# One ready semaphore in place of two, and three edits to the order of work, in the last stage of a two-block transformer kernel

## The chip, the cores and the metric

The kernel runs on one core of a Trainium2 chip. The metric is the device time of one execution in microseconds (us).

The core has five engines with queues of their own: PE (matrix products; PEld is its weight load), DVE (vector work), ACT (activations and copies), POOL (further elementwise work, and here the issuer of transfers that add into memory) and SP (transfers). Each engine takes its instructions in order. They wait for each other by semaphores.

## The reference

x has 32 batches of 256 tokens of 128 features. Four blocks follow each other, each on the layernorm of x, each added to x: causal attention with 16 heads, a mixture of 16 experts, attention on hyperbolic distance, and a two-layer MLP. The change touches the last two:

```python
def _hyperbolic_distance(q, k, c):
    q_norm_sq = jnp.sum(q * q, axis=-1, keepdims=True)
    k_norm_sq = jnp.sum(k * k, axis=-1)[..., None, :]
    qk = jnp.einsum('bhnd,bhmd->bhnm', q, k)
    diff_sq = q_norm_sq + k_norm_sq - 2.0 * qk
    denom = (1.0 - c * q_norm_sq) * (1.0 - c * k_norm_sq)
    denom = jnp.maximum(denom, 1e-06)
    cosh_arg = 1.0 + 2.0 * c * diff_sq / denom
    cosh_arg = jnp.maximum(cosh_arg, 1.0)
    return jnp.arccosh(cosh_arg)
...
dist = _hyperbolic_distance(q, k, CURVATURE)
attn = jax.nn.softmax(-dist, axis=-1)
out = jnp.einsum('bhnm,bhmd->bhnd', attn, v)
...
h = jax.nn.relu(jnp.einsum('bsd,dw->bsw', x, w1) + b1)
return jnp.einsum('bsw,wd->bsd', h, w2) + b2
```

## The kernel before

Three stages run one after the other: causal attention, experts, and then hyperbolic attention with the MLP, in `hyperbolic_attention_and_mlp`. Only this last one changes. x stays in on-chip memory throughout.

The stage goes over the 32 batches. In each batch the 16 heads are taken as 8 pairs p = 0 to 7. One pair's matrix is 128 x 1024 numbers.

- Rows: DVE and ACT build feature rows from q and k (`dve_lo`, `dve_features`); PE turns them per pair (`pe_turn_rows`, L1362, "row r" below); ACT or DVE copies the result to `rowsT` (`copy_rows`, L1497), ACT for pairs 0 and 3.
- Products: `pe_pairs` (L1371) makes two products per pair from rowsT, the squared distance in `d_ps` and the inverse of the denominator in `i_ps`. Each is four matmuls of few rows, 28 for d and 6 for i, in different row groups of PE.
- DVE reads them: `dve_distances` (L1636) clamps d_ps into a ring `u` of 12 pairs, `dve_ratio` (L1641) multiplies by i_ps.
- The argument of arccosh then needs a square root. For pairs 0 to 5 POOL forms the product u(u + 2) in `spare` (`pool_product`, L1557 to L1560) and ACT takes its root (`act_roots`, L1504); for pairs 6 and 7 ACT takes two roots itself (L1508, L1509). POOL issues a transfer that adds the root into u (`pool_sum`, L1550). ACT takes logarithm and exponential one batch later (`act_weights`, L1517 and L1520), and PE multiplies with the values (`pe_values`, L1395).
- The output is normalised, projected and added to x two to three batches later (`pe_turn_o`, `dve_normalise`, `pe_project`, `dve_residual`). The MLP of a batch runs four to five batches later: `pool_norm4` (L1573) normalises x, `pe_turn_x4` (L1435) turns it, ACT copies both turned inputs at once (`act_both_xT`, L1478, "the xTs copy"), `pe_hidden` (L1445) makes the hidden layer in two halves, `act_relu` (L1545), `pe_y` (L1456) and `dve_y` (L1682).

No planner orders this. Each engine has a body per batch, written out by hand: a loop over p, with the other work hung on certain values of p. On PE, DVE and ACT batches 0 to 5 are written out, batches 6 to 29 are a hardware loop of three batches per pass, and 30 and 31 are written out again. POOL's list is written out in full. Constants say at which p the work stands: `HIDDEN_AT` for the two halves of the hidden layer, `SUMS_BEHIND` for the products behind which POOL issues the sums, and `BUSY_AHEAD` and `BUSY_BEHIND` for `pe_keep_busy` (L1424), products without use that go to a part of o_ps that is free.

In PE's body, at each p, come first the products of the next pair, then what else hangs on p. In the first step these are turn_x, turn_x4, rows 5 and 6, and at the end y. In ACT's body come a row copy, the xTs copy, the logarithms and exponentials of the batch before by pairs of p, with feature copies and relu between, and then the roots of this batch. A change of table (ACT_TABLE_LOAD) stands ahead of each half.

Of the kernel before, what the change touches and what calls it, by code (L numbers as in the profile page):

```python
# [23 lines left out]
TB = N // P  # L24
# [1210 lines left out]
def hyperbolic_attention_and_mlp(nc, io, keep, y_dram, batches):  # L1235
# [9 lines left out]
    RING = 12  # L1245
    TURN = 3
    PRODUCTS = (0, 1, 2, 3, 4, 5)
    SUMS_BEHIND = {5: (0, 1, 2, 3, 4, 5, 6, 7)}
    ROWS_BY_SCALAR = (0, 3)
    EARLY_ROWS = 5  # L1250
    VALUES_AT = (2, 3, 4, 5)
    BACK_AT, ATTN_AT, PROJECT_AT = 4, 6, 7
    HIDDEN_AT = (1, 3)
    BUSY_AHEAD, BUSY_BEHIND = {5: 1}, {4: 4, 7: 1}
    HW = WB // 2
    NORM_BEHIND, NORM4_BEHIND = 2, 5
    with ExitStack() as stack:
# [46 lines left out]
        xh_done, xh_turned, xT_done, qkv_ready = S_("xh_done3"), S_("xh_turned3"), S_("xT_done3"), S_("qkv_ready")  # L1304
        hi_done, qkv_taken = S_("hi_done"), S_("qkv_taken")
        norm2_done, gap_done = S_("norm2_done"), S_("gap_done")
        sides_done, inverse_done, masked_far_done = S_("sides_done"), S_("inverse_done"), S_("masked_far_done")
        inv_hi_done, rows_done, rows_turned, rowsT_done = S_("inv_hi_done"), S_("rows_done"), S_("rows_turned"), [S_(f"rowsT_done{n}") for n in range(2)]
        d_ready, i_ready, dist_done, u_done = S_("d_ready"), S_("i_ready"), S_("dist_done"), S_("u_done")
        raised = S_("raised")  # L1310
        prod_done, root_done, ln_done, w_done, pv_done = S_("prod_done"), S_("root_done"), S_("ln_done"), S_("w_done"), S_("pv_done3")
        sum_landed = [S_(f"sum_landed{n}") for n in range(HP)]
# [51 lines left out]

        def pe_pairs(pe, b, p, i):

            def products(ps, r0, n):
                for j in range(TB):
                    for e in range(2):
                        at = slice(e * PITCH + r0, e * PITCH + r0 + n)  # L1370
                        last = nc.tensor.matmul(ps[:, e * W2 + j * N:e * W2 + (j + 1) * N],  # L1371
                                                rowsT[at, slot(i, p), 1, j * P:(j + 1) * P],
                                                rowsT[at, slot(i, p), 0, :],
                                                start=True, stop=True)
                return last

            pe.wait_ge(rowsT_done[p % 2], b * (HP // 2) + p // 2 + 1)
            after(pe, dist_done, b * HP + p)
            products(d_ps, 0, DROWS).then_inc(d_ready, 1)
            after(pe, u_done, b * HP + p)  # L1380
            products(i_ps, IROW, IROWS).then_inc(i_ready, 1)

        def pe_values(pe, b, g, i):
            pe.wait_ge(w_done, b * HP + 2 * g + 2)
# [106 lines left out]

        def copy_rows(engine, b, p, i):
            engine.wait_ge(rows_turned, b * HP + p + 1)
            after(engine, i_ready, b * HP + p - RING + 1)
            dst = rowsT[:, slot(i, p), :, :].rearrange("p s n -> p (s n)")
            src = r_ps[p % 2][:, :]
            ins = nc.scalar.copy(dst, src) if engine is nc.scalar else nc.vector.tensor_copy(dst, src)  # L1497
            ins.then_inc(rowsT_done[p % 2], 1)
# [112 lines left out]
        def dve_features_end(dve, b):  # L1611
            vec = nc.vector
            dve.wait_ge(inverse_done, b + 1)
            vec.tensor_tensor(inverse, whole.unsqueeze(1).to_broadcast([P, 2, TB, 2, H]), signs[:, :, :, :, :], ALU.mult
                              ).then_inc(masked_far_done, 1)
            dve.wait_ge(masked_far_done, 2 * b + 1)
            for a in range(2):
                ins = vec.scalar_tensor_tensor(out=far[:, a, :, :], in0=signs[:, 1 - a, :, 1, :], scalar=BIG,
                                               in1=inverse[:, a, :, 1, :], op0=ALU.mult, op1=ALU.add)
            ins.then_inc(masked_far_done, 1)  # L1620
            at = lambda side, n: rows[:, side, :, :, IROW + n:IROW + n + 4:3]
            near = inverse[:, :, :, 0, :].rearrange("p a t h -> p t h a")
            there = far[:, :, :, :].rearrange("p a t h -> p t h a")
            vec.tensor_copy(at(0, 0), near)
            vec.tensor_copy(at(0, 1), near)
            dve.wait_ge(masked_far_done, 2 * b + 2)
            vec.tensor_copy(at(1, 0), there)
            vec.tensor_copy(at(1, 2), there).then_inc(inv_hi_done, 1)
            dve.wait_ge(inv_hi_done, b + 1)
            vec.tensor_tensor(at(0, 2), near, at(0, 0), ALU.subtract)  # L1630
            vec.tensor_tensor(at(1, 1), there, at(1, 0), ALU.subtract).then_inc(rows_done, 1)

        def dve_distances(dve, b, p, i):
            dve.wait_ge(d_ready, b * HP + p + 1)
            after(dve, pv_done, b * GROUPS + p // 2 - RING // 2 + 1)
            nc.vector.tensor_scalar(u[:, slot(i, p), :], d_ps[:, :], 0.0, None, ALU.max).then_inc(dist_done, 1)  # L1636

        def dve_ratio(dve, b, p, i):
            dve.wait_ge(i_ready, b * HP + p + 1)
            dve.wait_ge(dist_done, b * HP + p + 1)  # L1640
            nc.vector.scalar_tensor_tensor(out=u[:, slot(i, p), :], in0=i_ps[:, :], scalar=1.0 / DEN_MIN,  # L1641
                                           in1=u[:, slot(i, p), :], op0=ALU.min, op1=ALU.mult).then_inc(u_done, 1)
# [66 lines left out]
        with nc.Block() as block:  # L1709
            @block.tensor  # L1710
            def _(pe):
# [8 lines left out]
                def body(b, i, one_before, two_before, three_before, four_before, five_before, one_after, two_after):  # L1720
                    for p in range(HP):
                        following = next_pair(b, p, one_after)
                        if following:
                            pe_pairs(pe, *following, i if p + 1 < HP else (i + 1) % TURN)
                        if one_after and p == 0:
                            pe_turn_x(pe, b + 1)
                        if four_before and p == 0:
                            if not one_after:
                                pe.wait_ge(res_done, b - 2)
                            pe_turn_x4(pe, b - 4, (i - 4) % TURN, misc, N)  # L1730
                        if one_after and p == 1:
                            pe_qkv(pe, b + 1, 0)
                        for r in {0: (5, 6), 1: (7,)}.get(p, ()):
                            pe_turn_rows(pe, b, r)
                        if four_before and p == HIDDEN_AT[1]:
                            pe_hidden(pe, b - 4, 1, (b + 1) * (HP // 2))
                        if one_before and p in VALUES_AT:
                            pe_keep_busy(BUSY_AHEAD.get(p, 0))
                            pe_values(pe, b - 1, VALUES_AT.index(p), (i - 1) % TURN)
                        if one_after:  # L1740
                            if p == 2:
                                pe_qkv(pe, b + 1, 1)
                            for r in {5: (0,), 6: (1,), 7: (3,)}.get(p, ()):
                                pe_turn_rows(pe, b + 1, r)
                        if two_before:
                            if BACK_AT <= p < BACK_AT + TB:
                                pe_turn_o(pe, b - 2, p - BACK_AT, (i - 2) % TURN, b + 2 if one_after else batches)
                            if p == ATTN_AT:
                                pe_turn_attn(pe, b - 2)
                            if p == PROJECT_AT:  # L1750
                                pe_project(pe, b - 2)
                        if one_after:
                            for r in {6: (2,), 7: (4,)}.get(p, ()):
                                pe_turn_rows(pe, b + 1, r)
                        if one_before:
                            if p == HP - 1:
                                pe.wait_ge(o_copied, 2 * b)
                            pe_keep_busy(BUSY_BEHIND.get(p, 0))
                        if five_before and p == 0:
                            pe_y(pe, b - 5, 2 * (b - 1))  # L1760
                        if four_before and p == HIDDEN_AT[0]:
                            if not one_after:
                                pe.wait_ge(late_xT4_done, 1)
                            pe_hidden(pe, b - 4, 0, (b + 1) * (HP // 2))
                over_batches(pe, body)

                after(pe, res_done, END - 1)
# [138 lines left out]
            def _(dve):  # L1906
# [9 lines left out]
                def body(b, i, one_before, two_before, three_before, four_before, five_before, one_after, two_after):  # L1916
                    for p in range(HP):
# [4 lines left out]
                        dve_ratio(dve, b, p, i)  # L1922
                        if p == 0 and three_before:
                            dve_residual(dve, b - 3)
                        for r in {0: (4,), 1: (5, 6), 2: (7,)}.get(p, ()):
                            copy_rows(dve, b, r, i)
                        if p == 1 and five_before:
                            dve_y(dve, b - 5)
                        if p == 3 and three_before:
                            dve_stats(b - 3, i)  # L1930
                        if p == 4 and three_before:
# [163 lines left out]
```

## Time and profile before

| | |
|---|---|
| median of 3 runs | 2494.11 us (2487.18 to 2496.76) |
| the profiled execution | 2494.11 us; its span 2492.1 us, 2.0 us around it |
| third stage | from about 1338 us to the end |
| granted TensorE clock, mean | 0.91 of 2.4 GHz |
| busy over the whole span | PE 86%, DVE 78%, ACT 71%, POOL 65% |

A row of the timeline has the start in us, the duration in us, engine, line, operation, output and inputs with shapes, the number of instructions merged, and in brackets the idle time ahead of it with what ended it. Two long instructions of one engine overlap by about 0.1 us at their ends, so the starts, not the durations, give the pace. A row of a window has its ends and length, the busy time and instructions of PE, PEld, DVE, ACT and POOL, the granted clock as a share of 2.4 GHz, the busy share of the transfer engines and GB/s. "issue" is idle time for which the profile shows no semaphore.

### The profile page before, as it was taken

Reading aid. Unit: us, or ns where it says so; the run is one execution under the profiler, and the core shown is the slowest. Engines: PE = TensorE matmul, PEld = TensorE weight load, DVE = VectorE, ACT = ScalarE, POOL = GpSimd, SP = SyncE. Lnnn points to the kernel's source line nnn. Section 1 sums busy time; section 2 is a strip of 40 time slices with the busy share of each in tenths; the row PEclk is TensorE's granted clock in tenths of the full one; section 3 lists DMA queues with packets and bytes.
Section 4 is the critical chain, followed back from the end, with each engine's and each line's share of the span. In section 5 each row is a group of like instructions: output and inputs, shape, how many; then the busy total and the mean of one; then the engine's idle time right before and its main releaser. Section 6 shows DMA issues by size and latency. Waiting matters only on the chain. (4 is left out here: it accounts for less than half of the span.)

```text
span 2492.1 us, 50814 instructions
## 1 busy us (share of the span) xinstructions
PE 2147.4 (86%) x15438; PEld 1607.4 (64%) x15438; DVE 1950.1 (78%) x5939; ACT 1767.7 (71%) x3085; POOL 1626.9 (65%) x1866
## 2 busy tenths in 40 slices
PE   4999999999999988999996778877878787787876
PEld 3677777777777767888884445555555555554554
DVE  4677777777777765787776899988989898898982
ACT  2666666666666653444423999989889898998995
POOL 2766676676667730000005999989889898888992
PEclk7999999999999997999995788988889898888887
DMA  5000000000000004534430667756576566755674
GB/s 140 1 2 2 2 1 2 2 1 2 1 2 1 2 1 91 116 69 104 103 69 19 131 132 140 140 111 126 113 139 127 112 123 126 139 108 113 128 140 78
DMA packets 81422, 184.53 MB, mean 74 GB/s; under 512 B 9478, under 2 KB 31529, under 8 KB 81194
## 3 DMA queue, kind: packets, MB, share of 16 engines
q0 software_dynamic: 36864, 134.23, 28.7%
q1 hardware_dynamic: 36010, 43.38, 7.6%
q10 hardware_dynamic: 8320, 4.19, 0.7%
q8 instruction: 103, 1.69, 0.3%
q14 instruction: 125, 1.02, 0.1%
HBM read 42.85 MB, written 4.72 MB: 19 GB/s over the span
## 5 line engine op out<-in xcount | busy, mean ns | idle before, releaser
L1560 POOL TENSOR_TENSOR spare<-spare,u 128x1024 f32<-128x1024 f32 x192 | 456.0, 2375 | 16.0
L542 ACT ACTIVATE prob<-s_ps,nmax 128x128 f32<-128x128 f32 (+1 forms) x1024 | 364.3, 432 | 132.2 <-DVE nmax L599 132.2
L599 DVE CUSTOM_DVE_ANT_0 s_ps<-s_ps,mask 128x128 f32<-128x128 f32 (+1 forms) x1024 | 340.6, 385 | 100.6 <-issue 76.4
L1641 DVE SCALAR_TENSOR_TENSOR u<-i_ps,u 128x1024 f32<-128x1024 f32 x256 | 313.6, 1225 | 60.2 <-issue 31.9
L579 POOL TENSOR_TENSOR g_lo<-g_all,g_hi 128x512 fp32r<-128x512 f32 x256 | 329.2, 1286 | 21.4
L1636 DVE TENSOR_SCALAR u<-d_ps 128x1024 f32<-128x1024 f32 x256 | 311.3, 1216 | 34.4 <-PE d_ps L1371 32.2
L534 ACT COPY g_all<-g_ps 128x512 f32<-128x512 f32 x256 | 151.5, 592 | 161.2 <-PE g_ps L63 160.2
L1517 ACT ACTIVATE u<-u 128x1024 f32<-128x1024 f32 x256 | 257.0, 1055 | 3.5 <-DMA u<-spare 3.5
L1520 ACT ACTIVATE u<-u 128x1024 f32<-128x1024 f32 x256 | 255.5, 1050 | 0.0
L991 POOL TENSOR_TENSOR x_lo<-xTs,x_hi 128x512 fp32r<-128x512 f32 x16 | 21.8, 1360 | 326.9 <-ACT x_hi L987 326.9
L475 PE MATMUL t_ps<-ident,prob 128*128 128x128 f32 x1536 | 232.1, 274 | 1.6 <-ACT pT L609 1.2
L1395 PE MATMUL o_ps<-u,v 128*32 128x256 f32 x2048 | 157.5, 431 | 86.3 <-ACT u L1520 85.7
L1550 POOL DMA_DIRECT2D u<-spare x256 | 228.3, 1402 | 4.6 <-ACT u L1509 2.1
L475 PEld LDWEIGHTS t_ps<-ident,prob 128*128 128x128 f32 x1536 | 192.1, 141 | 55.6 <-ACT prob L542 2.0
L1362 PE MATMUL r_ps<-ident,rows 128*128 128x128 f32 x1024 | 186.0, 320 | 38.9 <-ACT rowsT L1497 30.9
L1371 PE MATMUL i_ps<-rowsT 6*128 6x256 f32 x1024 | 139.9, 354 | 92.2 <-DVE u L1641 91.4
L1558 POOL TENSOR_SCALAR spare<-u 128x1020 f32<-128x1020 f32 x192 | 215.8, 1124 | 0.0
L1159 ACT ACTIVATE act_g<-eg_ps 128x512 f32<-128x512 f32 x128 | 76.3, 598 | 189.8 <-PE eg_ps L63 189.7
L61 PE MATMUL s_ps<-g_hi,x_hi 128*128 128x512 f32 x384 | 188.6, 491 | 20.5 <-issue 16.7
L612 DVE COPY pT<-t_ps 128x512 f32<-128x512 f32 x256 | 176.6, 690 | 33.5 <-PE t_ps L475 27.2
L555 POOL TENSOR_TENSOR g_hi<-g_all,ones 128x4 fp32r<-128x4 f32 x256 | 51.6, 202 | 221.7 <-ACT g_all L534 218.2
L1504 ACT ACTIVATE spare<-spare 128x1024 f32<-128x1024 f32 x192 | 188.5, 1045 | 5.3 <-POOL spare L1560 5.3
(275 smaller groups left out, 5658.2 us busy)
## 6 DMA issues: line engine op xcount, KB each, us to landing
u<-spare POOLq DMA_DIRECT2D x256, 512.0 KB, 11.9
w_all<-w_rows SPq DMA_DIRECT2D x128, 256.0 KB, 5.9
x<-L_attn_x ACTq DMA_DIRECT2D x8, 512.0 KB, 13.9
y<-x SPq DMA_DIRECT2D x32, 128.0 KB, 9.9
wkqv<-L_attn_Wkqv SPq DMA_DIRECT2D x4, 528.0 KB, 8.7
gate_rows<-L_ffn_gate_proj SPq DMA_DIRECT2D x1, 512.0 KB, 14.4
up_rows<-L_ffn_up_proj SPq DMA_DIRECT2D x1, 512.0 KB, 11.5
down_cols<-L_ffn_down_proj SPq DMA_DIRECT2D x1, 512.0 KB, 13.2
```

The costliest lines, as they stand in the source:

```text
L61: nc.tensor.matmul(out, hi, other_hi, start=True, stop=False)
L475: last = nc.tensor.transpose(t_ps[s % 2][:, c * P:(c + 1) * P], prob[:, s % 3, c, :], keep.ident)
L542: last = nc.scalar.activation(prob[:, kind, at, :].rearrange("p c n -> p (c n)"), s_ps[kind][:, at.start * P:at.stop * P], ACT.Exp, bias=n ...
L579: nc.gpsimd.tensor_tensor(g_lo[:, gb, q, :], g_all[:, h % 2, :], g_hi[:, gb, q, :], ALU.subtract).then_inc(g_split, 1)
L599: last = nc.vector.tensor_tensor_reduce(out=scores, in0=scores, in1=keep.mask[:, N - width:N], scale=-1.0, scalar=3.4e38, op0=ALU.add, op1 ...
L1517: nc.scalar.activation(pair, pair, ACT.Ln, bias=1.0 if whole else 0.0).then_inc(ln_done, 1)
L1520: nc.scalar.activation(pair, pair, ACT.Exp, scale=-1.0 if whole else -2.0).then_inc(w_done, 1)
L1550: nc.gpsimd.dma_start(u[:, slot(i, p), :], spare[:, p, :], accum_op=ALU.add).then_inc(sum_landed[p], 16)
L1558: nc.gpsimd.tensor_scalar(extra[:, 4:2 * W2], pair[:, 4:2 * W2], 1.0, 2.0, ALU.mult, ALU.add).then_inc(raised, 1)
L1560: nc.gpsimd.tensor_tensor(extra, extra, pair, ALU.mult).then_inc(prod_done, 1)
L1636: nc.vector.tensor_scalar(u[:, slot(i, p), :], d_ps[:, :], 0.0, None, ALU.max).then_inc(dist_done, 1)
L1641: nc.vector.scalar_tensor_tensor(out=u[:, slot(i, p), :], in0=i_ps[:, :], scalar=1.0 / DEN_MIN, in1=u[:, slot(i, p), :], op0=ALU.min, op1= ...
```

## The change

The pair's two ready semaphores, `d_ready` and `i_ready`, become one, `pair_ready`. PE waits for both readers, `dist_done` and `u_done`, before the first of a pair's eight matmuls, and issues them in an order that takes the four row groups in turn. DVE waits once per pair, ahead of the distances. One semaphore that counted two events (`masked_far_done`) becomes two. POOL issues the sums of pairs 0 and 1 behind product 4 and not behind product 5. PE makes the first half of the hidden layer in step 2, ahead of the values, and no longer at the end of step 1. DVE does `dve_y` ahead of the copies of rows 5 and 6. The products without use become 10 calls per batch from 6.

```diff
-    SUMS_BEHIND = {5: (0, 1, 2, 3, 4, 5, 6, 7)}
+    SUMS_BEHIND = {4: (0, 1), 5: (2, 3, 4, 5, 6, 7)}
...
-    HIDDEN_AT = (1, 3)
-    BUSY_AHEAD, BUSY_BEHIND = {5: 1}, {4: 4, 7: 1}
+    HIDDEN_AT = (2, 3)
+    BUSY_AHEAD, BUSY_BEHIND = {3: 1, 5: 1}, {4: 6, 7: 2}
...
         def pe_pairs(pe, b, p, i):
 
-            def products(ps, r0, n):
-                for j in range(TB):
+            pe.wait_ge(rowsT_done[p % 2], b * (HP // 2) + p // 2 + 1)
+            after(pe, dist_done, b * HP + p)
+            after(pe, u_done, b * HP + p)
+            for j in range(TB):
+                for ps, r0, n in ((d_ps, 0, DROWS), (i_ps, IROW, IROWS)):
                     for e in range(2):
                         at = slice(e * PITCH + r0, e * PITCH + r0 + n)
                         last = nc.tensor.matmul(ps[:, e * W2 + j * N:e * W2 + (j + 1) * N],
                                                 rowsT[at, slot(i, p), 1, j * P:(j + 1) * P],
                                                 rowsT[at, slot(i, p), 0, :],
                                                 start=True, stop=True)
-                return last
-
-            pe.wait_ge(rowsT_done[p % 2], b * (HP // 2) + p // 2 + 1)
-            after(pe, dist_done, b * HP + p)
-            products(d_ps, 0, DROWS).then_inc(d_ready, 1)
-            after(pe, u_done, b * HP + p)
-            products(i_ps, IROW, IROWS).then_inc(i_ready, 1)
+            last.then_inc(pair_ready, 1)
...
         def dve_distances(dve, b, p, i):
-            dve.wait_ge(d_ready, b * HP + p + 1)
+            dve.wait_ge(pair_ready, b * HP + p + 1)
...
         def dve_ratio(dve, b, p, i):
-            dve.wait_ge(i_ready, b * HP + p + 1)
             dve.wait_ge(dist_done, b * HP + p + 1)
...
-                        if four_before and p == HIDDEN_AT[1]:
-                            pe_hidden(pe, b - 4, 1, (b + 1) * (HP // 2))
+                        if four_before and p in HIDDEN_AT:
+                            if not one_after:
+                                pe.wait_ge(late_xT4_done, 1)
+                            pe_hidden(pe, b - 4, HIDDEN_AT.index(p), (b + 1) * (HP // 2))
...
+                        if p == 1 and five_before:
+                            dve_y(dve, b - 5)
                         for r in {0: (4,), 1: (5, 6), 2: (7,)}.get(p, ()):
                             copy_rows(dve, b, r, i)
-                        if p == 1 and five_before:
-                            dve_y(dve, b - 5)
```

## Rows read from the trace of the kernel before

**Rows 1.** Busy time of each engine by window, one per pass of the loop.
```profile
1536.50:1636.60 100.10, 81.24 (x664) 55.81 (x662) 92.39 (x183) 96.25 (x124) 95.15 (x94) 0.93 0.69 131
...
1742.30:1848.10 105.80, 84.64 (x654) 58.79 (x654) 93.01 (x183) 96.25 (x124) 94.59 (x93) 0.89 0.65 123
1848.10:1952.20 104.10, 81.80 (x654) 56.40 (x654) 92.84 (x183) 96.19 (x125) 95.51 (x95) 0.92 0.66 125
...
sum 839.00, PE 670.04 PEld 463.22 DVE 745.18 ACT 770.00 POOL 760.78; mean PE 83.76 PEld 57.90 DVE 93.15 ACT 96.25 POOL 95.10
```

**Rows 2.** The same, one window per batch, between ACT's table loads.
```profile
1636.64:1675.76 39.12, 29.56 (x223) 20.62 (x224) 32.81 (x64) 32.12 (x42) 31.68 (x32) 0.87 0.59 112
1675.76:1708.35 32.59, 27.12 (x210) 18.80 (x210) 30.75 (x62) 32.02 (x42) 31.68 (x32) 0.88 0.70 133
1708.35:1742.33 33.98, 27.79 (x223) 19.27 (x222) 29.44 (x59) 32.12 (x42) 31.67 (x32) 0.91 0.67 127
```

**Rows 3.** Waits, 1500 to 2400 us: total us, times, longest.
```profile
ACT xTs L1478 <- PE misc L1435: 44.5, 14, 4.5
...
DVE u L1641 <- issue: 31.9, 7, 4.9
```

**Rows 4.** Timeline of DVE around the loop's jump back.
```profile
1633.08 1.22 DVE L1636 TENSOR_SCALAR u<-d_ps 128x1024 f32<-128x1024 f32 x1
1639.15 1.23 DVE L1641 SCALAR_TENSOR_TENSOR u<-i_ps,u 128x1024 f32<-128x1024 f32 x1 [4.86 <-issue]
```

**Rows 5.** One pass, 1638.9 to 1744.5: instruction packets; instructions of L1640.
```profile
q14 instruction: 5, 0.04, 0.1%
...
L1640 DVEq EVENT_SEMAPHORE  x24: 21/21/50, 1639.1 to 1736.4; - x24
```

**Rows 6.** Timeline of ACT, 1675 to 1712 us.
```profile
1690.25 1.99 ACT L1520 ACTIVATE u<-u 128x1024 f32<-128x1024 f32 x2
...
1697.55 4.83 ACT L1504 ACTIVATE spare<-spare 128x1024 f32<-128x1024 f32 x5
...
1702.75 1.05 ACT L1504 ACTIVATE spare<-spare 128x1024 f32<-128x1024 f32 x1
...
1710.67 0.59 ACT L1478 COPY xTs<-misc 128x512 f32<-128x512 f32 x1 [1.04 <-PE misc L1435]
```

**Rows 7.** Timeline of POOL, 1625 to 1712 us.
```profile
1672.10 2.79 POOL L1573 TENSOR_SCALAR xh<-x,part_mv,rstd 128x127 f32<-128x127 f32 x2
...
1694.16 2.36 POOL L1560 TENSOR_TENSOR spare<-spare,u 128x1024 f32<-128x1024 f32 x1
1696.85 0.20 POOL L1557 TENSOR_TENSOR spare<-u,twos 128x4 f32<-128x4 f32 x1 [0.33 <-DVE u L1641]
...
1700.47 5.31 POOL L1550 DMA_DIRECT2D u<-spare  x6
1704.69 2.78 POOL L1573 TENSOR_SCALAR xh<-x,part_mv,rstd 128x127 f32<-128x127 f32 x2
```

**Rows 8.** Timeline of PE, 1675 to 1698 us.
```profile
1675.91 0.38 PE L1435 MATMUL misc<-ident,xh 128*128 128x128 f32 x2
...
1677.00 1.95 PE L1456 MATMUL o_ps<-w,hidden 128*128 128x128 f32 x16
1678.88 0.39 PE L1371 MATMUL d_ps<-rowsT 28*128 28x256 f32 x2
...
1679.12 0.28 PE L1371 MATMUL i_ps<-rowsT 6*128 6x256 f32 x2
...
1693.90 3.55 PE L1424 MATMUL o_ps<-qkvoT,ident 128*128 128x256 f32 x8
```

**Rows 9.** Timeline of DVE in the same batch.
```profile
1678.46 1.28 DVE L1497 CAST rowsT<-r_ps 128x512 fp32r<-128x512 f32 x2
1679.65 0.41 DVE L1682 TENSOR_TENSOR x<-o_ps,x 128x256 f32 x1
...
1686.12 0.48 DVE L1668 BATCH_NORM_STATS2 part_stats<-x 128x6 f32 x2
```

More of the change, by code:

```diff
@@ L1306, in hyperbolic_attention_and_mlp @@
         norm2_done, gap_done = S_("norm2_done"), S_("gap_done")
-        sides_done, inverse_done, masked_far_done = S_("sides_done"), S_("inverse_done"), S_("masked_far_done")
+        sides_done, inverse_done, masked_done, far_done = S_("sides_done"), S_("inverse_done"), S_("masked_done"), S_("far_done")
         inv_hi_done, rows_done, rows_turned, rowsT_done = S_("inv_hi_done"), S_("rows_done"), S_("rows_turned"), [S_(f"rowsT_done{n}") for n in range(2)]
-        d_ready, i_ready, dist_done, u_done = S_("d_ready"), S_("i_ready"), S_("dist_done"), S_("u_done")
+        pair_ready, dist_done, u_done = S_("pair_ready"), S_("dist_done"), S_("u_done")
         raised = S_("raised")
@@ L1493, in copy_rows @@
             engine.wait_ge(rows_turned, b * HP + p + 1)
-            after(engine, i_ready, b * HP + p - RING + 1)
+            after(engine, pair_ready, b * HP + p - RING + 1)
             dst = rowsT[:, slot(i, p), :, :].rearrange("p s n -> p (s n)")
@@ L1614, in dve_features_end @@
             vec.tensor_tensor(inverse, whole.unsqueeze(1).to_broadcast([P, 2, TB, 2, H]), signs[:, :, :, :, :], ALU.mult
-                              ).then_inc(masked_far_done, 1)
-            dve.wait_ge(masked_far_done, 2 * b + 1)
+                              ).then_inc(masked_done, 1)
+            dve.wait_ge(masked_done, b + 1)
             for a in range(2):
@@ L1619, in dve_features_end @@
                                                in1=inverse[:, a, :, 1, :], op0=ALU.mult, op1=ALU.add)
-            ins.then_inc(masked_far_done, 1)
+            ins.then_inc(far_done, 1)
             at = lambda side, n: rows[:, side, :, :, IROW + n:IROW + n + 4:3]
@@ L1625, in dve_features_end @@
             vec.tensor_copy(at(0, 1), near)
-            dve.wait_ge(masked_far_done, 2 * b + 2)
+            dve.wait_ge(far_done, b + 1)
             vec.tensor_copy(at(1, 0), there)
@@ L1760, in body @@
                             pe_y(pe, b - 5, 2 * (b - 1))
[L1761 to L1764, printed above, removed]
                 over_batches(pe, body)
```

## The prediction

> **What bounds the kernel now.** I read the share of busy time by stretch first. The change touches only the third stage, 1338 to 2492 us. Of its 32 batches, b = 6 to 29 run in a hardware loop of three batches per pass, eight passes in 839.0 us [rows 1]. The first pass, which is entered without a jump back, takes 100.1 us; six of the other seven take 105.7 to 105.9 us and one 104.1 (of the eight rows the first, the third and the fourth stand). In a pass ScalarE (ACT) is busy 96.3 us, GpSimd (POOL) 95, VectorE (DVE) 93. So three engines are each near the length of the undisturbed pass, and none has much to give. Split by batch [rows 2], the batch behind the jump takes 39.12 us, the next 32.59, the third 33.98; ACT needs 32.0 to 32.1 in each. An undisturbed batch is therefore ACT's own work, end to end.
>
> Then the waits [rows 3]. DVE sits 31.9 us, seven times, at L1641 for "issue", that is for no semaphore. ACT waits 44.5 us for the transposes in front of its xTs copy, the largest part of it behind those seven. The DVE timeline shows the place [rows 4]: the last instruction of the pass starts at 1633.08, the first of the next pass only at 1639.15, 4.86 us idle. This is the jump back of DVE's loop. The DMA view has 5 instruction packets of 8 KB in one pass [rows 5], so the loop is fetched anew each pass. The compiled DVE loop has 340 instructions of 64 bytes, a packet carries 128. By the instruction that DVE had reached when each packet started, I place block edges at about its 57th, 185th and 313th instruction: the loop lies in four blocks, and its first block is gone when the jump wants it. ACT's loop (233 instructions) shows no such wait [rows 3].
>
> Last, the timelines of one undisturbed batch, all times from its row of ACT's second pair of exponentials, which ends at 1692.24 [rows 6]. POOL is busy without a gap but 0.3 us [rows 7].
>
> **The change part by part.**
>
> *The merged ready semaphore.* Each ratio loses one wait. The compiled list has a separate wait instruction in front of each of the 24 ratios of a pass [rows 5]; 18 of them vanish (six hold another wait too), and 42 vanish in the six batches written out ahead of the loop. The loop shrinks to 322 instructions and starts 42 earlier, so the edges move to about its 99th and 227th, and the third falls behind its end: three blocks in place of four. With the next block prefetched that makes four held at the jump. I take it that the 4.86 us stall goes. It is bounded by a pass without a jump: 105.8 - 100.1 = 5.7 us for six jumps and 104.1 - 100.1 = 4.0 for one, 38 us [rows 1]; I count 38. The lower bound of this gain is 0, if the block is lost all the same.
>
> The other side of the merge: PE now starts the d products of the next pair only when DVE's ratio has read i_ps. PE waits there anyway for the i products, so what follows on PE is not later: eight products together take about 0.5 us where both waits are met [rows 8], as four i products alone. For DVE the distances can start some 0.6 us after the ratio. In six of the eight steps a row copy or longer work lies between (two copies take 1.28 us); at p = 3 it is 0.48 us of statistics, at p = 5 about as much, so 0.1 to 0.2 us show [rows 9]. They are covered by the new DVE slack below; I count 0, and 0.3 x 26 = 8 us without that cover.
>
> *SUMS_BEHIND.* This is the costly edit. POOL's sums of pairs 0 and 1 move in front of its product 5. A sum waits for the root of its pair. Product 4 ends at 1696.5; root 0 starts at 1697.55 and, one of five in 4.83 us, ends at about 1698.6, root 1 at 1699.55 [rows 6, 7]. POOL now stands still 2.1 us, issues sum 0, waits for root 1, issues sum 1 (0.6 to 0.7 us each by six in 4.2), and only then multiplies. Product 5 used to run 1696.85 to 1700.5, now about 1700.3 (0.2 to 0.6 us more while descriptors are written) to 1704.4. Queued behind it on POOL: sums 2 to 5, norm4, sums 6 and 7, the products of the next batch. On ACT, root 5 stood at 1702.75 and must now wait until 1704.4: 1.7 us on the engine that sets the batch. On POOL, norm4 starts 3.9 us later less two sums already issued (1.4), so 2.5 us later; it ends at 1707.5 now, 1710.0 then. Its customer is turn_x4 on PE in the next batch's first step. In the batch before, norm4 was done at 1674.9 and turn_x4 ran at 1675.91 [rows 7, 8]: 1.0 us of slack, so 1.55 us remain, and PE's in-order queue behind it (rows 5 and 6, y, the next pair, qkv, hidden) and ACT's xTs copy go with it. The two delays run beside each other; the chain over PE and DVE is the longer. POOL stays out of the bound itself: its 31.7 us of work and the 2.1 us stand fit in 34.5.
>
> *dve_y ahead of the row copies.* y's products end at 1678.95 [rows 8]; DVE is through with the ratio of pair 1 at 1678.5 and used to copy two rows before y at 1679.65 [rows 9]. Now it waits 0.45 us for y with the copies behind it: distances 2 and all after, 0.5 us later. The last hidden product, and ACT's relu behind it, follow.
>
> *HIDDEN_AT.* Half 0 moves one step later on PE, into step 2. Half 1 remains behind pair 4. About 1.0 us of PE moves from a gap at p = 1 to p = 2, where qkv 1 comes about 1.5 us later than now, just as ACT reaches it. I count 0; without that cover 0.5 us a batch.
>
> *BUSY.* Four more calls a batch, two of them in step 4 on the way from the values to pair 6. The four there now take 3.55 us, most of it at the low clock [rows 8], so two more are 1.8 us, or about 1.0 at full clock. DVE gets distances 6 that much later, but by the first step of the next batch it waits for POOL's norm4 in any case (it would have 2 us of slack there). Count 0; bound 1.0 x 26 = 26 us. What they may give back is clock: 0.89 to 0.93 is granted in the passes shown [rows 1]. I count nothing, since PE also gets new waits.
>
> **The sum.** A fast batch: 1.55 + 0.5 = 2.05 us. In the third batch of a pass xTs already waits for a late PE (1.04 us at 1710.67), which hides part: 1.3. A pass: 2.05 + 2.05 + 1.3 = 5.4; eight passes +43. Jumps: -38. Batches 1 to 5, ACT nearly always at work there too: 1.5 x 5 = +7. Batches 30 and 31: +4; ACT's 1.7 us once more in the tail: +2. Sum +18, less 2 for clock kept up where the 5 us hole is gone: +16. The profiled execution itself took 2494.1 us (span 2492.1), which is also the median of the three runs. So 2510 us.
>
> **The rivals.**
>
> A. As above: jump cured, its gain eaten by the wait in front of product 5: 2485 to 2530.
>
> B. The jump still stalls. The edges are my reading and may lie some tens of instructions off, or the first block may be lost in any case. Then the 38 us are not won: about 2548. The Trainium skill, "Runtime: NRT & Kernel Launch", section "Instruction fetch mechanics", says that an engine holds two blocks of 256 instructions and that a taken branch out of this window costs a fetch. By that rule a loop of 322 can still reach over three blocks, and would then stay at this rival's time; the trace's packets are half that size.
>
> C. The end on the other side: POOL's stand before product 5 hides. It decides on one number: root 0 done at 1698.6 against product 4 at 1696.5. If POOL in steady state runs 2 us later against ACT, it does not stand, and what is left is two sums (1.3 us) ahead of product 5, which root 5 (2.2 us behind product 5's end now) takes without a wait. Then only y's 0.5 us x 26 = 13 us stands against 38: about 2470. For it: POOL is full in fast batches. Against: its cycle with the stand is still shorter than the chain's.
>
> D. The longer dummy work and the d products behind the ratio both show, with the low clock at every step 4: 26 + 8 on A: about 2544.
>
> **Numbers.** A 0.52, B 0.13, C 0.23, D 0.12. Half a per cent, 12.5 us, is what a measurement of this kernel can tell from none: 2481.6 to 2506.6. C is nearly all faster; of A 0.22 of the whole lies under 2506.6 with a little below 2481.6; the rest is slower. Faster 0.24, same 0.24, slower 0.52. Range 2470 to 2550: from C's time to B's. A's own is 2485 to 2530.
>
> **What would show it.** Stall: no "issue" idle at L1641 behind the jump, seven ACT waits of 4.5 us gone, passes all alike at 104 to 107 us. POOL: a new wait at L1550 for ACT's root of about 2 us in each batch, root 5 on ACT waiting 1 to 2 us for POOL. PE: turn_x4 waiting for POOL's norm4. DVE: y waiting about 2 us. Wrong: if passes are near 100 us (C), or show 4 us at the jump (B), or if DVE waits for d products far more than for y (D).

## The result: 3% slower, and the profile after

The change makes the kernel slower: 2568.57 us (median of 4 runs, 2557.45 to 2572.67) against 2494.95 us, ratio 1.0302, 95% interval 1.0263 to 1.034. Forecast were 2510 us and a range to 2550. The profiled execution took 2563.7 us, its span 2561.8. Two kernels below had one execution each in a slower state with a lower granted clock (a_hidden_back 3388 us, a_sums_back 3085 us); their ratios leave it out, and their medians would be at most 0.6 us lower without it.

Busy time by window, one per pass of the loop in the middle of the stage, answers to [rows 1]:

```profile
1653.23:1765.82 112.59, 91.28 (x679) 59.79 (x678) 93.59 (x184) 96.66 (x124) 94.77 (x94) 0.83 0.61 115
1765.82:1880.40 114.58, 92.48 (x674) 60.99 (x674) 93.15 (x183) 96.65 (x123) 94.75 (x94) 0.81 0.60 114
```

DVE, ACT and POOL do the same work as before (93, 96 and 95 us), but a pass takes 112.6 to 114.6 us and not 105.8; forecast were 104 to 107. PE's busy time grew from 84.6 to 91.3 us for 25 more instructions (the longer dummy work is 24 of them), and the granted clock is 0.83, not 0.89.

The waits, 1500 to 2450 us (total us, times, longest), answer to [rows 3]:

```profile
POOL u L1547 <- ACT spare L1501: 130.3, 26, 5.7
PE d_ps L1374 <- DVE u L1637: 116.5, 85, 2.4
DVE u L1633 <- PE i_ps L1374: 110.8, 67, 3.2
ACT rows L1485 <- PE misc L1350: 84.3, 25, 4.0
...
ACT spare L1501 <- POOL spare L1557: 40.7, 25, 3.5
DVE x L1678 <- PE o_ps L1453: 30.9, 26, 1.6
...
PEld misc L1432 <- POOL xh L1570: 2.4, 8, 0.3
```

DVE's idle time without a semaphore behind the jump [rows 3, 4] is gone from the list: the jump back is cured. But now ACT waits 3.4 us in each batch for qkv 1 (L1485), which it did not before, and DVE waits for pairs. The timeline of one batch shows where. PE first, from the end of step 1:

```profile
1729.61 1.95 PE L1453 MATMUL o_ps<-w,hidden 128*128 128x128 f32 x16
...
1732.75 0.66 PE L1362 MATMUL r_ps<-ident,rows 128*128 128x128 f32 x4
1735.83 0.58 PE L1374 MATMUL d_ps<-rowsT 28*128 28x256 f32 x2 [2.42 <-DVE u L1637]
...
1736.56 2.08 PE L1442 MATMUL r_ps<-xTs,w 128*128 128x256 f32 x4
1738.57 1.94 PE L1392 MATMUL o_ps<-u,v 128*32 128x256 f32 x16
1740.43 1.65 PE L1350 MATMUL misc<-qkvoT,xTs 128*128 128x384 f32 x2
```

Then the idle times that answer to it, one line each of the timelines of DVE, DVE, ACT, POOL and ACT:

```profile
1731.67 0.42 DVE L1678 TENSOR_TENSOR x<-o_ps,x 128x256 f32 x1 [1.06 <-PE o_ps L1453]
1742.73 1.23 DVE L1633 TENSOR_SCALAR u<-d_ps 128x1024 f32<-128x1024 f32 x1 [3.01 <-PE i_ps L1374]
1742.12 0.38 ACT L1485 ACTIVATE rows<-misc 128x256 fp32r<-128x256 f32 x1 [3.54 <-PE misc L1350]
1754.70 1.80 POOL L1547 DMA_DIRECT2D u<-spare  x2 [5.27 <-ACT spare L1501]
1760.21 1.06 ACT L1501 ACTIVATE spare<-spare 128x1024 f32<-128x1024 f32 x1 [1.55 <-POOL spare L1557]
```

DVE stands 1.06 us for y with two copies behind it, so pair 2 is late. PE stands 2.42 us for it with nothing to do, because the half of the hidden layer that used to fill this place has moved behind pair 3. Then pair 3, the half, values 0 and qkv 1 come one behind the other, each at nearly twice its time: 2.08, 1.94 and 1.65 us, where the same matmuls take 1.13, 1.07 and 0.91 in the kernel a_y_back (rows below). The windows of the hole and of what follows say why (the granted clock is the third number from the end):

```profile
1733.40:1735.80 2.40, 0.01 (x1) 0.00 (x1) 2.37 (x3) 2.40 (x6) 2.32 (x4) 0.91 1.06 201
1735.80:1742.00 6.20, 6.17 (x30) 2.81 (x30) 3.82 (x8) 2.78 (x3) 6.12 (x6) 0.50 0.77 153
```

0.50 is the lower level, 1.2 GHz. The batch is a typical one: between 1500 and 2420 us the hole is 2.42 us in all 25 batches, and from pair 3 to the end of qkv 1 PE takes 6.2 to 6.3 us in 22 of them and 4.8 to 5.0 in three.

### The profile page after: what moved, and what is told of

The parts are those of the page before. It is cut to its first block and busy times, and to the rows that moved or that the text cites. A ratio compares the mean times of both kernels' runs of the same rounds, so it can differ in the third digit from the quotient of the medians.

```text
span 2561.8 us, 51304 instructions
## 1 busy us (share of the span) xinstructions
PE 2204.0 (86%) x15686; PEld 1621.7 (63%) x15686; DVE 1956.0 (76%) x5939; ACT 1771.0 (69%) x3085; POOL 1622.4 (63%) x1866
## 3 DMA queue, kind: packets, MB, share of 16 engines
q0 software_dynamic: 36864, 134.23, 27.8%
## 5 line engine op out<-in xcount | busy, mean ns | idle before, releaser
L1374 PE MATMUL d_ps<-rowsT 28*128 28x256 f32 x1024 | 148.1, 367 | 160.0 <-DVE u L1637 157.1
L1374 PEld LDWEIGHTS d_ps<-rowsT 28*128 28x128 f32 x1024 | 94.3, 216 | 260.7 <-issue 256.2
L1392 PE MATMUL o_ps<-u,v 128*32 128x256 f32 x2048 | 170.3, 460 | 68.3 <-ACT u L1517 67.8
L1555 POOL TENSOR_SCALAR spare<-u 128x1020 f32<-128x1020 f32 x192 | 228.2, 1189 | 0.0
L1421 PE MATMUL o_ps<-qkvoT,ident 128*128 128x256 f32 x620 | 208.1, 480 | 0.0
```

Of the source, the lines that this page charges most:

```text
L1421: nc.tensor.matmul(o_ps[:, N:2 * N], keep.ident, keep.qkvoT[:, 0:2, :], start=True, stop=True, skip_group_check=True)
```

## Experiments

Theories ahead of the first runs. H: the moved half makes most of the loss. S: POOL's stand behind product 4 does. M: the merged wait, the dummy work or y does. "Before" ran at 2490.8 to 2492.4 us beside every group of kernels below, so their times are compared directly. Beside the changed kernel itself it ran at 2494.95, so differences to the changed kernel are uncertain by some 3 us more. Names that begin with a_ are the changed kernel with something put back; those with p_ are the kernel before with 72 extra instructions ahead of DVE's list (below, "the padded base") and one or more parts of the change added; those with b_ or m_ are what their sections say.

### Each part put back alone

```diff
 a_hidden_back
-    HIDDEN_AT = (2, 3)
+    HIDDEN_AT = (1, 3)
 a_sums_back
-    SUMS_BEHIND = {4: (0, 1), 5: (2, 3, 4, 5, 6, 7)}
+    SUMS_BEHIND = {5: (0, 1, 2, 3, 4, 5, 6, 7)}
 a_busy_back
-    BUSY_AHEAD, BUSY_BEHIND = {3: 1, 5: 1}, {4: 6, 7: 2}
+    BUSY_AHEAD, BUSY_BEHIND = {5: 1}, {4: 4, 7: 1}
```

> The changed kernel, with the first half of the hidden layer back at the end of PE's step 1. Theory H (the moved half is the main loss: it leaves a hole on PE at the end of step 1, the granted clock falls there, and pair 3, the half, the values and qkv 1 then run at the low clock in front of ACT's copy of qkv 1 and pair 4): 2500 to 2530 us, 40 to 65 under the changed kernel, ACT's 3.5 us wait for qkv 1 gone. Theory S (POOL's stand for root 0 is the main loss): within 15 us of the changed kernel, 2555 to 2570. Theory M (the merged wait, the dummy work or y's place is the main loss): the same as S here.

Measured: 2503.07 us, 65.5 under the changed kernel; ratio to before 1.0037 (1.0016 to 1.0058). As H said.

> The changed kernel, with all sums behind product 5 again. Theory H: the 5 us stand of POOL for root 0 goes, but little of the time, 2550 to 2568. Theory S: most of the loss goes, 2500 to 2530. Theory M: 2555 to 2570.

Measured: 2541.95 us, 26.6 under the changed kernel (1.0201, 1.0179 to 1.0222). Between H's and S's figures: a second cause, not the main one. ACT's wait for qkv 1 stays (81.0 us, 26 times).

> The changed kernel, with the dummy work of the kernel before (6 calls a batch, not 10). Theory H and theory S: 2545 to 2575, a few us either way by the clock. Theory M, if the dummy work in step 4 is what holds PE: 25 to 50 us less, 2520 to 2545.

Measured: 2572.01 us, 3.4 over the changed kernel (1.0323, 1.0306 to 1.0341). In the changed kernel the longer dummy work costs nothing in all. Why stands under "Parts together".

### The jump alone, and a base without it

```diff
+        pad = m.sb("pad", [P, 80])
...
+                for k in range(72):
+                    nc.vector.memset(pad[:, k:k + 1], 0.0)
                 dve.wait_ge(zeroed, 4)
                 for j in range(TB):
                     dve_lo(dve, 0, j, 0)
```

> The kernel before, with 72 one-element memsets on DVE ahead of the whole stage's list and nothing else, so that the DVE loop of 340 instructions starts 72 instructions later and lies in three blocks of 128 by my reading of the edges. If the jump's cost hangs on the blocks that the loop touches: the 4.9 us idle behind the jump goes, passes of about 100 to 101 us, 2450 to 2462 in all. If it hangs on the length of the loop, or the first block is lost in any case: 2490 to 2500 as before.

Measured: 2441.82 us, ratio 0.9793 (0.9775 to 0.9812): 49 us under before, by 72 instructions more, and 8 us under the range given. DVE's timeline over the jump answers to [rows 4], with no idle time:

```profile
1630.16 1.28 DVE L1498 CAST rowsT<-r_ps 128x512 fp32r<-128x512 f32 x2
1631.36 1.22 DVE L1637 TENSOR_SCALAR u<-d_ps 128x1024 f32<-128x1024 f32 x1
```

A pass, as a window:

```profile
1634.93:1733.91 98.98, 81.34 (x655) 55.88 (x656) 92.97 (x183) 96.15 (x123) 95.02 (x94) 0.91 0.69 131
```

The opposite test puts 60 such instructions into the changed kernel, so that its shorter loop straddles a fourth block.

> The changed kernel with 60 one-element memsets on DVE ahead of the stage's list, so that by my reading of the edges its loop of 322 instructions lies in four blocks again. If the edges decide: 4 to 5 us idle on DVE behind the jump, and 30 to 50 us more, 2598 to 2620. If the shorter loop was what cured the jump: 2560 to 2575.

Measured: 2586.32 us (1.0386, 1.0359 to 1.0412), 17.8 over the changed kernel and between the two ranges. The stall is back, 27.4 us in seven jumps, but costs less than I expected, since the passes hold other waits that take some of it up. DVE's timeline at the first jump, and its waits:

```profile
1648.84 1.21 DVE L1634 TENSOR_SCALAR u<-d_ps 128x1024 f32<-128x1024 f32 x1
1653.84 1.22 DVE L1638 SCALAR_TENSOR_TENSOR u<-i_ps,u 128x1024 f32<-128x1024 f32 x1 [3.78 <-issue]
```

```profile
DVE u L1638 <- issue: 27.4, 7, 5.3
```

So where the loop lies decides, not its length: 340 instructions run through, 322 stall. The merge cured the jump by moving and shortening the list, not as a semaphore. The transfer view agrees: between 1550 and 2300 us the instruction queue moves 43 packets in the kernel before and 39 in a_pad60, but 9 in b_pad72 and 9 in the changed kernel. The loop is fetched anew in each pass only where it stalls. None of the kernels below changes the count of DVE's instructions, and none of their traces shows the stall.

### Each part alone on the padded base

The edits are those of the change (the reverse of the diffs above; y as in the change's own diff).

> The padded kernel before (2441.8 us) with the first half of the hidden layer moved to step 2, nothing else of the change. Putting it back took 65 us off the changed kernel. If the move costs this alone, whatever stands beside it: 2495 to 2520 us, PE's low clock in step 2 and ACT's wait for qkv 1 of 2 to 4 us in each batch. If it costs only together with the merged wait or the sums (which make PE and ACT late already): 2440 to 2460.

Measured: 2460.20 us, +18.4 (ratio to before 0.9876, 0.986 to 0.9893). At the upper edge of the second range: alone it is a small part of the loss. What the half covers shows in the padded base, where PE makes it and then waits 0.60 us for pair 2's ratio (0 to 0.6 us in the other batches):

```profile
1672.12 1.03 PE L1446 MATMUL r_ps<-xTs,w 128*128 128x256 f32 x4
...
1674.19 0.50 PE L1372 MATMUL i_ps<-rowsT 6*128 6x256 f32 x4 [0.60 <-DVE u L1642]
```

With the half moved, PE's timeline in a batch:

```profile
1745.39 0.50 PE L1372 MATMUL d_ps<-rowsT 28*128 28x256 f32 x4 [0.52 <-DVE u L1637]
1746.72 0.50 PE L1372 MATMUL i_ps<-rowsT 6*128 6x256 f32 x4 [0.82 <-DVE u L1642]
1747.15 1.28 PE L1446 MATMUL r_ps<-xTs,w 128*128 128x256 f32 x4
1748.36 1.93 PE L1396 MATMUL o_ps<-u,v 128*32 128x256 f32 x16
1750.22 1.49 PE L1351 MATMUL misc<-qkvoT,xTs 128*128 128x384 f32 x2
```

The same pattern, shorter: the hole is 0.52 us and then 0.82, and ACT waits 1.58 us for qkv 1, not 3.54. It does not wait in every batch: 23.9 us in 16 waits between 1500 and 2400 us.

> The padded kernel before with DVE's y ahead of the copies of rows 5 and 6, nothing else. The prediction's step gives 0.5 us a batch, 13 us: 2450 to 2458. If DVE's copies have slack: 2438 to 2446.

Measured: 2469.57 us, +27.8 (0.9914, 0.9898 to 0.9931), twice the forecast and over both ranges. DVE's wait for y is 0.53 us in the batch shown, but 0.92 in the mean of 27 batches, the longest 1.6 (24.8 us, against 6.6 in the padded base, 1500 to 2400 us). The second relu on ACT waits 1.22 us here, where in a batch of the padded base it waited 0.66; together ACT's relus wait 34.8 us and not 15.0:

```profile
1711.70 0.42 DVE L1683 TENSOR_TENSOR x<-o_ps,x 128x256 f32 x1 [0.53 <-PE o_ps L1457]
1721.11 0.60 ACT L1546 ACTIVATE hidden<-r_ps 128x512 f32<-128x512 f32 x1 [1.22 <-PE r_ps L1446]
```

> The padded kernel before with the sums of pairs 0 and 1 behind product 4, nothing else. The prediction's own step gives 1.55 us a batch or 43 us: 2475 to 2490. What putting them back gave in the changed kernel, 27 us: 2460 to 2475. If POOL's stand hides: 2438 to 2447.

Measured: 2475.95 us, +34.1 (0.9947, 0.9928 to 0.9966). In the first range. POOL stands for the root (1.3 to 3.7 us, 1.9 in the mean) and ACT's root 5 for POOL (42.2 us in 26 waits):

```profile
1765.09 1.81 POOL L1551 DMA_DIRECT2D u<-spare  x2 [1.88 <-ACT spare L1505]
1770.60 1.06 ACT L1505 ACTIVATE spare<-spare 128x1024 f32<-128x1024 f32 x1 [1.56 <-POOL spare L1561]
```

> The padded kernel before with the dummy work of the change (10 calls a batch), nothing else. In the changed kernel the longer dummy work was worth nothing measurable, 3 us. The same here: 2438 to 2447. If it holds PE on the way to pair 6 in an undisturbed kernel: 2450 to 2470. If the clock it keeps up is worth something: 2425 to 2436.

Measured: 2479.56 us, +37.7 (0.9947, 0.9921 to 0.9972), over all three ranges and over the prediction's bound of 26. PE behind step 4 (twelve products, six calls), PE behind step 7 (four products, two calls, ahead of the next batch's first step), and ACT, which has to wait for the turned inputs:

```profile
1732.88 3.04 PE L1425 MATMUL o_ps<-qkvoT,ident 128*128 128x256 f32 x12
...
1745.69 1.73 PE L1425 MATMUL o_ps<-qkvoT,ident 128*128 128x256 f32 x4
```

```profile
1748.64 0.59 ACT L1479 COPY xTs<-misc 128x512 f32<-128x512 f32 x1 [1.20 <-PE misc L1436]
```

In the mean of the batches, the products behind step 4 take 3.0 us here and 2.5 in the padded base (there 1.9 to 3.5), and those behind step 7 take 1.7 and 0.9. ACT's waits for the turned inputs grow from 8.3 to 29.8 us and those of the relus from 15.0 to 21.5.

```diff
 b_merge: the changed kernel with half, sums, dummy work and y all put back
```

> The changed kernel with all four edits of the order (hidden half, sums, dummy work, y) put back, so that of the change only the merged ready semaphore stands; its DVE loop lies in three blocks. By the prediction (merge costs nothing beside the jump's gain): 2438 to 2450, as the padded kernel before. If PE's d products behind the ratio show on every pair, as DVE's waits for pairs in the changed kernel (111 us in all) suggest: 2465 to 2500.

Measured: 2450.39 us, +8.6 (0.9832, 0.9812 to 0.9852), at the top of the first range and far under the second. The merge as such costs what the prediction gave as its price without cover, 8 us; DVE's waits for pairs are 32.3 us and not 21.5 (1500 to 2400 us).

### Parts together

> The merged semaphore and the hidden half in step 2, the other three edits of the order put back. The merge alone ran 2450.4 us; the half alone cost 18.4 us on the padded kernel before, but 65 in the changed kernel. If the costs simply add: 2466 to 2472. If the half costs more because of the merge (PE now waits for DVE's ratio ahead of all eight products of pair 3, with the half, the values and qkv 1 behind them): 2482 to 2510.

Measured: 2462.06 us (0.9878, 0.9861 to 0.9895), 11.7 over b_merge and a little under the first range. Merge and half do not make each other worse.

> The padded kernel before with the hidden half in step 2 and DVE's y ahead of the copies, nothing else. Alone they cost 18.4 and 27.8 us. If the costs simply add: 2484 to 2492. If the half costs more because DVE's y makes pair 3 late in the same step: 2502 to 2530.

Measured: 2501.92 us (1.0037, 1.0018 to 1.0056), +60.1 on the padded base, where the two alone add to 46.2. At the lower edge of the second range: they make each other worse, by 14 us.

> The changed kernel with DVE's y behind the copies again. If y only adds its own 27.8 us: 2537 to 2545. If y and the hidden half make each other worse: 2495 to 2525. If other waits take its place: 2555 to 2570.

Measured: 2487.47 us (0.9984, 0.9972 to 0.9996): 81.1 under the changed kernel, more than any range given. One line of DVE's order takes the change from 3% slower to level with before. H in its first form falls: the half is not the largest part, y is as much of it. In this kernel the half is still in step 2, and PE still stands ahead of pair 3:

```profile
1750.78 0.38 PE L1374 MATMUL d_ps<-rowsT 28*128 28x256 f32 x2 [1.73 <-DVE u L1637]
...
1751.22 1.13 PE L1442 MATMUL r_ps<-xTs,w 128*128 128x256 f32 x4
1752.28 1.07 PE L1392 MATMUL o_ps<-u,v 128*32 128x256 f32 x16
1753.28 0.91 PE L1350 MATMUL misc<-qkvoT,xTs 128*128 128x384 f32 x2
```

The same hole and the same work as windows:

```profile
1749.00:1750.80 1.80, 0.07 (x5) 0.05 (x4) 1.77 (x3) 1.80 (x5) 1.80 (x3) 1.00 1.06 200
1750.80:1754.40 3.60, 3.39 (x30) 1.67 (x30) 3.50 (x7) 3.60 (x5) 3.52 (x4) 1.00 1.05 205
```

Behind a hole of 1.73 us the clock stays at 1.00 and the thirty matmuls take 3.6 us; behind one of 2.42 us, in the changed kernel, it is 0.50 and they take 6.2 us. ACT's wait for qkv 1 is no longer among the waits of this batch. Here too the batch is typical: the hole is 1.4 to 1.74 us in 26 batches, and up to the end of qkv 1 PE takes 3.4 us in 22 of them and 4.8 to 5.0 in four.

Two kernels looked for the rest of the loss:

> The merged semaphore, the hidden half in step 2 and DVE's y ahead of the copies; sums and dummy work as in the kernel before. Merge and half together ran 2462, the half and y without the merge 2502 (from a base of 2442). If the merge adds only its own 8.5 us to the half and y: 2503 to 2512. If merge, half and y together make the missing part of the loss (the edits alone and by pairs add to about 100 us, the whole is 127): 2530 to 2548.

Measured: 2503.62 us (1.0048, 1.0033 to 1.0062), 1.7 over p_hy. The merge adds nothing to half and y. In this kernel PE's hole ahead of pair 3 is 2.42 us in every batch, as in the changed kernel, but the work from pair 3 to the end of qkv 1 takes 5.0 us and not 6.25.

> The padded kernel before with all four edits of the order (half, y, sums, dummy work) and the two ready semaphores as they were. If the missing part needs the merge: 2525 to 2540 by the sum of the single costs and the pair half and y. If it is among the four edits: 2555 to 2570, no more than 10 under the changed kernel.

Measured: 2569.73 us (1.0297, 1.0269 to 1.0327), 1.2 over the changed kernel. All of the loss is in the four edits of the order; with them the merge costs nothing.

Four of the kernels now differ only in the sums and the dummy work, all with merge, half and y as in the change:

| | dummy work of before | dummy work of the change |
|---|---|---|
| sums of before | 2503.62 (m_hy) | 2541.95 (a_sums_back) |
| sums of the change | 2572.01 (a_busy_back) | 2568.57 (the change) |

On top of m_hy the dummy work costs 38.3 us, as it does alone. The sums cost 68.4, twice their 34.1 alone. Once the sums stand, the dummy work costs nothing. The trace of a_busy_back shows what it covers:

```profile
1730.02 0.44 PE L1432 MATMUL misc<-ident,xh 128*128 128x128 f32 x2 [0.89 <-POOL xh L1570]
1730.48 1.85 PE L1362 MATMUL r_ps<-ident,rows 128*128 128x128 f32 x8
1732.12 2.88 PE L1453 MATMUL o_ps<-w,hidden 128*128 128x128 f32 x16
...
1739.27 0.38 PE L1374 MATMUL d_ps<-rowsT 28*128 28x256 f32 x2 [2.42 <-DVE u L1637]
```

```profile
DVE x L1678 <- PE o_ps L1453: 90.5, 26, 3.9
...
ACT rows L1485 <- PE misc L1350: 65.6, 26, 4.0
```

Turn_x4 waits for POOL's norm4 (19.7 us in 23 waits), rows and y behind it run partly at the low clock, and DVE waits 90.5 us for y, where in the changed kernel it waits 30.9. With the two calls behind step 7 of the change, PE is busy while norm4 finishes, turn_x4 does not wait, and y takes 1.95 us and not 2.8. By these rows, what that saves is lost again behind it: from pair 3 to the end of qkv 1 the changed kernel takes 6.25 us where a_busy_back takes 4.7 to 5.0 in most batches, and ACT waits 84.3 us for qkv 1 and not 65.6.

### A better version

> The padded kernel before with DVE's y one step later, ahead of the copy of row 7 in step 2, the other way from the change. In the padded kernel DVE still waits 0.3 us for y in front of the distances of pair 2 in some batches. If that wait is on the way of ACT's relu: 2430 to 2440. If the place two copies behind is late enough already: 2440 to 2450.

Measured: 2469.75 us, +27.9 (0.99, 0.9865 to 0.9935). Moving y the other way costs as much as the change's way, and lies over both ranges. In the trace PE's values now wait for DVE to have read y out of o_ps (14.0 us in 27 waits, 1500 to 2400 us), and ACT waits longer for the turned inputs (25.6 us against 8.3) and ahead of the relus (27.3 against 15.0).

```diff
-    BUSY_AHEAD, BUSY_BEHIND = {5: 1}, {4: 4, 7: 1}
+    BUSY_AHEAD, BUSY_BEHIND = {5: 1}, {4: 2, 7: 1}    p_less4
+    BUSY_AHEAD, BUSY_BEHIND = {5: 1}, {4: 4}          p_no7
```

> The padded kernel before with two calls of dummy work behind step 4 in place of four (4 calls a batch in all). Two calls more there and two elsewhere cost 38 us on this base. If the cost is one of PE's time ahead of pair 6: 2425 to 2440. If four calls are few enough that they hide: 2438 to 2446. If their clock is needed for what follows: 2450 to 2480.

Measured: 2438.04 us (0.9796, 0.9769 to 0.9824).

> The padded kernel before without the one call of dummy work behind step 7. With two calls there ACT waited 1.2 us for the turned inputs in each batch. If PE's time ahead of turn_x4 still shows with one: 2428 to 2440. If it hides: 2438 to 2446. If the clock in the first step falls without it: 2450 to 2480.

Measured: 2441.89 us (0.9809, 0.9783 to 0.9835). Neither can be told from the padded base. The three calls taken out here, of the six of the kernel before, are hidden, and their clock is not needed. Which of the four added calls costs the 38 us, these two do not tell. The best version is therefore the kernel before with its DVE loop moved by 72 instructions, 2.1% faster than before, 4.9% faster than the change (2441.82 / 2568.57 = 0.951).

## Why the prediction was wrong

The parts, in us on the padded base (2441.8) and, taken out again, in the changed kernel (2568.6):

| part | counted | alone | saved by taking it out of the change |
|---|---|---|---|
| jump | -38 | -49.0 | -17.8 (a_pad60) |
| sums | +41 | +34.1 | 26.6 |
| y | +13 | +27.8 | 81.1 |
| half | 0, 13 without cover | +18.4 | 65.5 |
| dummy work | 0, bound 26 | +37.7 | -3.4 |
| merged wait | 0, bound 8 | +8.6 | -1.2 (against p_all) |
| half and y together | +13 | +60.1 | |
| all but the jump | +54 | +126.8 (change against base) | |

(The prediction's 5.4 us a pass is sums and y together, 43 us in eight passes; with its 7 + 4 + 2 for the ends, less 2 for the clock, the edits come to 54. I split them by 0.5 us x 26 for y.)

In one order of adding, each step measured on top of the ones before it: jump -49.0 (counted -38), half and y +60.1 (counted 13), merge +1.7 (0), sums +68.4 (41), dummy work -3.4 (0). What a part costs depends on which others stand, so no single column of the table is the price.

**The jump.** Right in mechanism, and mis-sized: 49 us in place of 38. The passes with the stall gone take 99.0 us, not the 100.1 of the first pass that I measured against [rows 1]. Rival B is out: the four places of the loop (before, padded, changed, changed and padded) stall and run as my blocks of 128 say, 4, 3, 3 and 4 of them.

The Trainium skill, "Runtime: NRT & Kernel Launch", section "Instruction fetch mechanics", has an engine hold two blocks of 256 instructions. I set this against the change in rival B, and wrongly: if every second of my edges is an edge of 256, they fall at about the 57th and 313th instruction of the old loop (three blocks), the 99th of the changed one (two), the 241st of the padded one (two) and the 39th and 295th of the changed and padded one (three). Two held blocks of 256 then give the same four answers. The runs do not tell the two readings apart, and the trace agrees with the page as well as with mine.

**SUMS_BEHIND.** Alone, the step is right nearly to the number: POOL's stand 2.1 forecast, 1.9 in the mean measured; root 5's wait 1.7 forecast, 1.6 measured; rival C (it hides) is out. The link over PE, turn_x4 waiting for norm4, was forecast as the longer of the two. In the full change it does not show (2.4 us in eight waits together, the longest 0.3), because the longer dummy work fills that place. With the short dummy work it does (a_busy_back, 19.7 us in 23 waits), and there the sums cost 68.4 us and not 41. In p_sums the loss goes mostly through ACT's root 5. The 5.3 us that POOL stands in the full change are a result of ACT being late: in a_y_back, with the same sums, POOL's stands add to 53.5 us and not 125.0 (1500 to 2400 us).

**y.** The mechanism was right, the size was not. The wait was read from one batch, 0.45 us; in p_y it is 0.53 in the shortest batches and 0.92 in the mean. The price follows the mean: 27.8 / 26 = 1.1 us a batch, not 0.5. What is late is all that PE has behind pair 3, and ACT's relu waits for the last of it (34.8 us against 15.0).

**HIDDEN_AT: the step that failed.** "About 1.0 us of PE moves from a gap at p = 1 to p = 2 [...] I count 0; without that cover 0.5 us a batch." I looked at when qkv 1 would come if only the half's own time moved. Two things were missing. In the undisturbed batch the half fills the place where PE waits for pair 2's ratio; taken away, the wait stands open. And the work behind pair 3 then often runs at the low clock. With y in front of the copies the hole grows from 1.73 to 2.42 us, and step 2's matmuls from 3.6 to 6.2 us. The 0.7 us and the 2.6 us together make most of the 3.5 us that ACT waits for qkv 1. Alone the half costs 18.4 us, with y 60.1 where 13 were counted. The failed assumption lies behind the whole sum too: "1.55 + 0.5" adds delays of single edits at a fixed clock, but half and y share one place, and the sums, on top of them, cost 68.4 us where 41 were counted.

**BUSY.** Counted 0 with a bound of 26; alone it is 37.7. My bound priced two calls behind step 4. The call behind step 7, right ahead of turn_x4, I did not price: it is the place of the 1.2 us wait of ACT above. In the full change it costs nothing, but not by the cover that I assumed: there it fills PE's wait for norm4 that the moved sums would open (a_busy_back). That my 0 comes out there is luck.

**The merged wait.** Right: 8.6 us alone against 8 without cover, and nothing measurable in the full change. Rival D's sign, DVE waiting for pairs far more than for y (110.8 against 30.9 us), did appear and misled: those waits are for the most part for pair 4 behind the slow step 2 (3.01 us in the batch shown), and no merged wait is needed for them (p_all has 105.7 us of them between 1500 and 2400 us).

**What stays open.** The clock's part is read from windows and matmul times of kernels that differ by one edit; no kernel held the clock up across the hole by itself (dummy work in that place was not tried), so the reading was argued from rows and not measured by itself. Nor does the length of the hole alone set the clock: in p_hidden it is low behind holes of 0.52 and 0.82 us, and behind the same 2.42 us step 2 takes 6.25 us in the changed kernel and 5.0 in m_hy. Nor does step 2 alone set the time: a_busy_back, with 4.7 to 5.0 us there in most batches, is no faster than the change. Half and y with sums and dummy work make 127.9 where p_hy's 60.1, 34.1 and 37.7 add to 131.9; that these agree is chance, since on top of half and y the sums cost twice as much and the dummy work nothing. No run has the sums and the dummy work without half and y.

## What to carry to other kernels

Price a move on an in-order queue by the hole that it leaves as well as by the work that it adds: look which engine's wait the moved piece was covering, and what all stands behind that wait. If another edit lengthens the same wait, price both together, and price PE's work behind the hole at the low clock as the other end of the range. Do not price an edit by taking it out of a kernel in which several others stand: here that gave 81 us for a part that costs 28 alone, and nothing for one that costs 38. Where a hardware loop shows idle time without a semaphore behind its jump, try moving its start before touching its body: here that alone was worth 2.1%, and every later edit that changes the number of instructions ahead of the loop can win or lose it again.

## What was not expected of the hardware

- Idle time of DVE behind the jump depends on the loop's place: 340 instructions at the old place 4.6 us on average (31.9 us in seven [rows 3]), the same 340 shifted by 72 none, 322 none, 322 shifted by 60 again 3.9 us on average (27.4 in seven). The stalling kernels move 43 and 39 instruction packets between 1550 and 2300 us, the others 9.
- A gap on PE of 1.73 us was followed by matmuls at clock 1.00 (a_y_back), one of 2.42 us in the same place by 0.50 for the next 6.2 us (the change). But the same 2.42 us were followed by 5.0 us of the same matmuls in m_hy, and in another kernel (p_hidden) matmuls at that place took 1.28, 1.93 and 1.49 us, partly or wholly at the low clock, behind gaps of only 0.52 and 0.82 us.
